# Where the 4-chunk transposes of h stand in TensorE's round: between two passes of the gates, or ahead of the next aggregation

## The reference, cut to what matters

```
adj = einsum('bn,tnm->btm', x.reshape(b, n*d), masker_param) + masker_bias     # b 2048, n 50, d 32, t 2
adj = relu(adj).reshape(b, t, n, n);  adj = adj / (adj.sum(-1) + 1e-6)
h = broadcast(x);  m = einsum('btnm,btmd->btnd', adj, h @ weight)
gates = m @ w_ih.T + b_ih + h @ w_hh.T + b_hh;  r, z, ng = split(gates, 3)
ng = tanh(sigmoid(r) * ng);  h = (1 - sigmoid(z)) * ng + sigmoid(z) * h
# batch norm of h over b, layer norm over (t, n, d), attention pooling over n
```

## Time and profile before

| What | us |
|---|---|
| median of 3 runs | 2270.66 |
| lowest run | 2262.55 |
| profiled execution, its own time | 2267.87 |
| its span in the trace | 2266.1 |
| PE busy | 2196.3 (97%) |
| DVE busy | 1086.5 (48%) |
| ACT busy | 961.4 (42%) |

### The profile page before, as it was taken

How to read it: one execution, slowest core, us unless ns; L and a number is a source line. 1 busy time by engine, 2 the same in 40 slices (tenths; PEclk the granted TensorE clock), 3 DMA queues, 4 the chain that set the end, 5 groups by cost and what they waited for, 6 DMA issues and landing times. The chain is left out here.

```text
span 2266.1 us, 34747 instructions
## 1 busy us (share of the span) xinstructions
PE 2196.3 (97%) x12302; PEld 1738.1 (77%) x12302; DVE 1086.5 (48%) x2177; ACT 961.4 (42%) x1639; POOL 135.4 (6%) x124
## 2 busy tenths in 40 slices
PE   8999999999999999999999999999999999986888
PEld 6888888888888888888888888777777777772333
DVE  4432233323335233322333133278888888884656
ACT  4322122212224122212222122278888888876551
POOL 0000000000000000000000000011101111004340
PEclk9999999999999999999999999999999999997899
DMA  6411222122224322122220223367676776746440
GB/s 215 154 54 64 94 91 90 29 93 90 90 91 144 107 91 93 43 77 91 95 89 28 93 93 72 103 166 197 187 198 180 194 193 183 200 150 194 119 119 5
DMA packets 341600, 264.00 MB, mean 116 GB/s; under 512 B 169318, under 2 KB 302854, under 8 KB 339846
## 3 DMA queue, kind: packets, MB, share of 16 engines
q1 hardware_dynamic: 323402, 225.63, 34.0%
q10 hardware_dynamic: 18144, 37.69, 5.1%
HBM read 195.59 MB, written 67.70 MB: 116 GB/s over the span
## 5 line engine op out<-in xcount | busy, mean ns | idle before, releaser
L443 PE MATMUL psum<-w_hi,x_lo 128*128 128x500 f32 x2080 | 821.2, 395 | 8.9 <-DVE w_lo L292 8.9
L443 PE MATMUL psum<-w_lo,x_hi 128*128 128x500 f32 (+1 forms) x2080 | 808.4, 389 | 0.0
L443 PE MATMUL psum<-w_hi,x_hi 128*128 128x500 f32 x1920 | 744.2, 388 | 0.0
L355 DVE TENSOR_REDUCE rows<-u 128x10 f32<-128x500 f32 x160 | 107.6, 673 | 889.6 <-ACT u L305 889.1
L443 PEld LDWEIGHTS psum<-w_hi,x_lo 128*128 128x128 f32 x2080 | 391.6, 188 | 83.7 <-issue 8.2
L443 PEld LDWEIGHTS psum<-w_lo,x_hi 128*128 128x128 f32 (+1 forms) x2080 | 391.9, 188 | 72.2
L443 PEld LDWEIGHTS psum<-w_hi,x_hi 128*128 128x128 f32 x1920 | 361.0, 188 | 73.0
L311 ACT COPY at<-psum 125x512 f32<-125x512 f32 x160 | 93.5, 585 | 676.4 <-PE psum L425 676.4
L305 ACT ACTIVATE u<-psum 128x500 f32<-128x500 f32 x160 | 93.8, 586 | 344.3 <-PE psum L443 344.3
L764 PE MATMUL psum<-adj_sb,xs_sb 100*64 100x100 f32 x2048 | 200.6, 350 | 1.6 <-PEq L145 1.6
L744 POOL TENSOR_TENSOR xg_lo<-xg_sb,xg_hi 128x400 fp32r<-128x400 f32 x64 | 67.0, 1050 | 1927.5 <-ACT xg_hi L593 1927.5
(11 more groups left out here) (162 smaller groups left out, 2277.8 us busy)
## 6 DMA issues: line engine op xcount, KB each, us to landing
w_raw<-W SPq DMA_DIRECT2D x140, 500.0 KB, 7.9
adjT<-at SPq DMA_DIRECT2D x160, 250.0 KB
adj_sb<-adjT SPq DMA_DIRECT2D x32, 1250.0 KB
xs_sb<-xz SPq DMA_DIRECT2D x16, 1600.0 KB
hF<-hC ACTq DMA_DIRECT2D x96, 256.0 KB, 6.5
h<-hF SPq DMA_DIRECT2D x64, 256.0 KB, 4.2
xg_sb<-xg ACTq DMA_DIRECT2D x14, 800.0 KB, 8.0
h<-hF SPq DMA_DIRECT2D x48, 192.0 KB, 3.5
```

The costliest lines, as they stand in the source:

```text
L355: nc.vector.tensor_reduce(rows[:, 0], u[:, c2], AX.X, ALU.add).then_inc(dve_step, 1)
L443: last = nc.tensor.matmul(mm_out(w % 2), a[0:r, w, k, :], b[0:r, k, :], start=k == 0 and n == 0, stop=k == KF and n == 1)
```

## The change

The call of `turn_chunks` leaves `gates` and stands at the head of the round in `turn`, in front of `aggregate(s + 1)`. What it issues, what it waits for and in which rounds it stands are the same. No other engine's order changes.

```
@@ gates
                 last.then_inc(rz_done, 1)
-                if q and (r or not (isinstance(it, int) and it == 0)):
-                    turn_chunks(it * 2 + r - 1, q - 1)
                 wait(pe, h_ready, it * S + s - 1)
@@ turn
                 for s in range(S):
+                    r, q = divmod(s, ROUNDS)
+                    if q and (r or not (isinstance(it, int) and it == 0)):
+                        turn_chunks(it * 2 + r - 1, q - 1)
                     if s + 1 < S or more:
                         aggregate((s + 1) % S)
                     gates(it, s, more)
```

## The result

The changed kernel took 2505.8 us (median of 6 runs) against 2267.2 us for the kernel before in the same comparison. The ratio is 1.106, with a 95% interval of 1.104 to 1.107; it is taken over the fast runs, without one of the six of the kernel before that took 4165.8 us. The forecast was 2453 us in a range of 2415 to 2520 us. Direction and loop came out as said, and 53 us more were lost than the sum had. They are rival (a), the clock, which had a chance of 0.14 and holds beside the loop. The bounds of the loop alone, 2422 to 2466 us, do not hold the measured time; the stated range does, because it took in half of that rival.

The account below looks back on a forecast made before the run. TensorE was taken to set the pace in stage 2. Six intervals of 1.91 us plus 0.85 at the border make 12.3 us a tile, 185 over 15 tiles, added to 2268: 2453 us, range 2415 to 2520.

Parts of the forecast that it names:

- loop: Stage 2, turns through aggregation, r and z pass, sigmoids and copy to next turns: 6.38 us against 4.47, 1.91 more.
- the sum: Stage 2: 12.3 us more a tile, times 15 tiles, 185 us more in all, giving 2453 us.
- rival (a): TensorE's idle time in the stage 2 rounds lowers its clock: up to 117 us more, 2570 us; chance 0.14.
- The bounds of the loop alone: Whole kernel: 2422 us if ScalarE's steps overlap by 0.3 us, 2466 us with the whole pause before the aggregation.
- The bound before: Stage 2 of the kernel before: TensorE sets the pace, with ACT busy 30.95 and DVE 30.40 of 35 us.
- Its cover: Today an aggregation and an r and z pass hide the copy's end, leaving 1.15 us before the next turns.
- The border: From round 7's turns to the next tile's first turns, waiting for hT: 9.1 us against 8.25, 0.85 more.
- the price of 1.3 us a round: Lower clock in a stage 2 round: 1.0 us more for the r and z pass, 0.3 us for the turns.
- the half for which 2511 us was given: Case in which half of the 90 stage 2 intervals run at the lower clock: 2511 us.
- (b): Rounds 1 and 2 wait only for block transposes, 27 us less saved pauses of 28: 2268 or 2295 us; chance 0.05.
- (c): A pause of 0.27 us saved on TensorE in each of 105 rounds, a faster kernel: 2240 us; chance 0.03.
- (d): Another slower course, such as ScalarE catching up part of the way: 2330 to 2410 us; chance 0.06.

Follow-up runs that it names:

- The run with the filler: The changed kernel plus eight extra matmuls behind the n pass in rounds 1 to 6 of a turned tile: 2451.6 us, ratio 1.082.
- first batch alone: The kernel before with only each tile's first batch of turns (round 1) at the head of the round: 2291.6 us, ratio 1.011.

## Why the prediction was right, and where it was short

**The bound before.** TensorE with little to spare on the others: right. Two of the kernels in which the loop is cut end within 1% of the kernel before.

**The loop.** 6.38 us was forecast and 6.36 is measured. Within it two errors cancel: the turns to the aggregation take 0.59 us (0.54 with the half pause), and the two sigmoids follow each other in 1.09, not 1.15. That the copy's position and the one bank make it is shown from three sides: the copy ahead of the sigmoids takes 226 of 239 us away, a second bank 203, and the wait alone, without any moved matmul, brings 137. The other 102 us are the longer loop (6.36 against 5.78 us, 90 times: 52 us), the border and more time at the lower clock.

**Its cover.** The 1.65 us by which the copy ended after the head of the next round was the right thing to look at. The wait on TensorE is 1.6 us and comes back every round, since the copy ends only after sigmoids that wait for the turns' own round.

**The border.** 9.1 us was forecast; at the full clock it is 9.3, and 10.18 in the changed kernel as it ran.

**The sum.** 185 us was forecast. The run with the filler, in which the clock reads 0.99 from 1500 to 2200 us, is 2451.6 us, 185 us over the kernel before in its comparison (2266.3). The sum of the forecast is thus what the loop costs, to within the 3 us that the clock still costs that run. That it agrees to the microsecond is luck. The step that fell short is the term of the clock, taken as zero in the sum: it measures 54 to 57 us.

**The clock, rival (a).** It had 0.14, with two windows of stage 3 that spoke against each other, and it is what happened. The prediction said that the clock should read 1.00 and that under 0.9 would show it wrong; the stage reads 0.87. So by its own sign the prediction is right on the loop and wrong on the clock, and the range held the time because it was widened for this rival. The one window that spoke against it held a single wait of 1.85 us, while here a wait of 1.6 us comes back every 6.4 us. But a wait need not come back in every round: with one longer wait a tile, for the block transpose, the clock fell in 5 of 15 tiles (0.99 us, two banks), in 3 (1.10 us, first batch alone) and in 3 (0.81 us, filler), and in none with 0.51 us (copy ahead). Why it fell behind these and not behind the 1.85 us is open. Of the price of 1.3 us a round, the 1.0 us for the r and z pass was right (0.99), and the 0.3 us for the turns was too much: a long interval costs 0.87 to 1.00 us in all. The number of rounds was three of six, as in the half for which 2511 us was given. That 2511 is near the measured 2506 is again in part luck, since the border, which that rival did not count, adds 0.9 us a tile: 3.7 us a tile, 56 us in 15.

The Trainium skill (TensorE: Matmul & The Clock Gate, A second HAM failure mode) describes kernels in which short idle times between groups of matmuls make the clock swing between its two levels. The trace agrees: 0.50 and 1.00 alternate within one tile.

**The other rivals.** (b), that only the block transposes are waited for, is false for the change, but what the first batch's wait costs can be seen in the run with that batch alone: 26 us, some 3 of them by the clock. (c), a saved pause, is false even with the loop cut: n pass and turns to the aggregation take 1.73 us, turns and n pass took 1.67. The pause ahead of the turns is there today, but none stands between turns and n pass, so moving the turns saves none: it only puts the pause ahead of the n pass. (d) did not occur.

## What to carry to other kernels

When a step is moved to the head of an in-order queue, its waits move too, and everything behind it waits with it: ask where the thing it waits for stands in the other engine's order, and whether that stands behind something that the moved step now delays. If so there is a loop, and its length can be added up from the rows of the timeline before anything is run: 6.38 for 6.36 us here, 5.84 for 5.78 and 4.75 for 4.87 in the experiments, and 9.1 for 9.3 over the border. Then ask how much idle time the loop leaves in TensorE in every round, because waits of 1.6 us in every round went with a lower clock here, and that was over a fifth of the loss (54 of 239 us). If a forecast rests on a clock of 1.00 while its own rows show such waits, that term needs a price in the sum and not only a wide range.

## What the runs showed of the hardware that was not expected

- The clock fell with waits of 1.6 us each 6.4 us: 0.87 on average, at 1.2 GHz about a quarter of the time. Eight fill-in matmuls a round (idle time left 0.2 us) brought it back to 0.99. In the run with two banks, where one longer wait of a tile is left, windows of 100 us read 0.98, and in 5 of 15 tiles the round behind that wait was at the lower level for part of its time.
- A lower clock did not lengthen everything. The aggregation's matmuls (100 × 64 by 100) took 1.55 us to the next pass at 0.50 (1724.68 to 1726.23, changed kernel) and 1.50 at 1.00; the first two aggregations of the kernel before took 2.98 us together at 0.50. The r and z pass took 2.28 us at 0.52 and 1.29 at 1.00.
- Weight loads of 128 × 128 behind others of 128 × 128 had no listed idle time between n pass and turns, in either order; between tiles of different size they had 0.26 to 0.29 us at the full clock, but 0.17 behind the turns. The number format did not decide it: from the aggregation to the turns, both plain fp32, it was 0.29 us, and from the turns to the n pass, of another format, none.
